# A graph attention kernel: VectorE's chain for the next chunk behind the second, third and fifth add, weights five groups ahead

## The chip, the cores and the metric

The kernel runs on one core of a Trainium2 chip. The metric is the device time of one execution in microseconds (us). The core has a matrix engine (TensorE, PE in the profile), a vector engine (VectorE, DVE), a scalar engine (ScalarE, ACT), a general engine that here mostly issues gathers (GpSimd, POOL) and an engine that issues transfers (SyncE, SP). They run their own instruction lists and meet at semaphores.

## What is computed

3125 nodes with 128 features, 50,000 edges sorted by their target node `dst`. First a layer norm and two plain graph convolutions, then a layer norm and five graph attention layers with two heads, each followed by relu but the last; both blocks add their input. Of the reference, the attention layer, which is where the change lies:

```python
def _gat_layer(x, src, dst, edge_attr_full, W, att, b, ew, eb):
    edge_emb = edge_attr_full @ ew.T + eb
    xw = x @ W
    xj = xw[src].reshape(-1, H, D) + edge_emb.reshape(-1, H, D)
    xi = xw[dst].reshape(-1, H, D)
    alpha = einsum('ehd,hd->eh', xi, att_i) + einsum('ehd,hd->eh', xj, att_j)
    alpha = leaky_relu(alpha, NEG_SLOPE)
    amax = segment_max(alpha, dst, num_segments=N)
    ea = exp(alpha - amax[dst])
    denom = segment_sum(ea, dst, num_segments=N)
    alpha = ea / (denom[dst] + EPS)
    msg = xj * alpha[..., None]
    aggr = segment_sum(msg, dst, num_segments=N)
    return aggr.mean(axis=1) + b
```

Every node also has an edge to itself, without attributes.

## The kernel before

The edges are cut into 391 tiles of 128 (one edge in each partition), the tiles into groups of four and the groups into chunks: 13 chunks of 28 tiles (seven groups), one of 16 and one of 11 tiles. That is 98 groups a layer and 490 in all. The 3125 nodes are 25 tiles.

**GpSimd** issues one indirect gather for each edge tile (L510): 128 rows of the layer's node table, picked by the edges' sources, go to one of 60 slots of `ring`. From the 60th tile on it first waits until TensorE has ended the group whose slot it fills (`sums`, L508). The gathers of a chunk count up one of five semaphores `gath`.

**TensorE** (`aggregate`) waits for a group's weights (`p_ready`), clears a bank with a zero matmul (L741) and multiplies each tile's gathered rows by the weighted one-hots `pw` (L745), and its edge attributes `est` by the plain one-hots (L747). The last one counts up `sums`. Behind the second, fourth and sixth group of chunks 0 to 7 (and the second of chunk 8) stands a self tile (L783): a node tile times the layer's weights, for the edges of nodes to themselves. It waits until VectorE has read the self tile before.

**VectorE** runs through a list that is written out by hand, chunk by chunk:
- `rescale` (L1185 to L1191) adapts the sums of the node that straddles two chunks;
- `add_group` (L1200), once for each group, waits for `sums` and adds a bank to the accumulators `acc`;
- `weigh` (L1161) makes the weights `pw` of a group that lies `AHEAD` groups further on in the same chunk;
- `self_rows` (L1215, L1216) takes a self tile out of its bank;
- the chain of the next chunk. `windows_sum` has three parts (L1087; L1091; L1093, L1094 and L1096). `chain_scan` (L1105 to L1123) waits until all gathers of the next chunk have landed, since it needs a column of the gathered rows, and forms the running maxima within 32 edges; `chain_rows` (L1129 to L1145) and `chain_cols` (L1150 to L1156) join them over the whole chunk; `chain_probs` (L1170 to L1175) waits for ScalarE's exponentials, writes `est` and weighs the next chunk's first two groups. At the end of a chunk `weigh` is called for the next chunk's groups 2 to `AHEAD`-1.

In `chain_at` stands behind which add of a chunk (counted from 0) the scan, the rows with the columns, and the probabilities go. There are six banks for the sums and six places for `pw` (`DEEP`).

**ScalarE** computes the exponentials (L586) and copies windows for the next chunk (L580). **SyncE** loads the attributes and the weights and stores the node table.

Of the kernel before, what the change touches and what calls it, by code (L numbers as in the profile page):

```python
# [49 lines left out]
GC = [[g for g in range(G) if GROUPS[g][0] == c] for c in range(NC)]  # L50
# [20 lines left out]
def s_tile_of(c, i):  # L71
    n = 3 * c + i // 2
    return n if c < 9 and i % 2 == 1 and i < 6 and n < NT else None
# [7 lines left out]
    return sum(not pool_group(k) for k in range(g + 1))  # L81


AHEAD = 4
SUM_BANKS = (0, 1, 2, 4, 5, 6)
DEEP = len(SUM_BANKS)


def chain_at(c):
    return (2, 3, 5) if len(GC[c]) >= 7 else (0, 1, len(GC[c]) - 2)  # L90


def in_class(c, layer):
# [4 lines left out]
def program(nc, x, src_rows, src_key, src_flat, dst_col, dst_next_col, dst_flat, dst_first,  # L98
            attr, W1, b1, W2, b2,
            weights, weightsT, attT, edge_w, edge_b, edge_woT, biases, edge_bias, out):  # L100
    with ExitStack() as ctx:
# [707 lines left out]
        def _(v):  # L809
# [7 lines left out]
            def link(ins):  # L817
                v.wait_ge(step, mark(ins))
# [110 lines left out]
            def weight_columns(layer):  # L929
                V.tensor_copy(Wl[:, layer % 2, H * D:H * D + H], V4[:, layer, 0:4:2]).then_inc(wv_sb, 1)  # L930
# [90 lines left out]
            for g in range(GCN_G):  # L1021
# [3 lines left out]
                c, i = divmod(g, K // GRP)  # L1025
# [55 lines left out]
            def windows_sum(layer, c, part):  # L1081
                gc, k, hk = layer * NC + c, CH[c], H * CH[c]
                ts = slice(TC[c], TC[c + 1])
                win, pr = ai_win[:, 0:k, :, :], prod[:, 0:hk * FA].rearrange("p (h k f) -> p h k f", h=H, f=FA)
                if part == 0:
                    v.wait_ge(at_in[gc % NAT], 16 * (gc // NAT + 1))
                    link(V.tensor_tensor(pr, at[:, gc % NAT, 0:k, :].unsqueeze(1).broadcast_to((P, H, k, FA)),  # L1087
                                         v17[:, layer, :, 0:FA].unsqueeze(2).broadcast_to((P, H, k, FA)), ALU.mult))
                if part == 1:
                    v.wait_ge(win_ready, gc + 1)  # L1090
                    link(V.tensor_tensor(win, win, onehot[:, ts, :].unsqueeze(2).broadcast_to((P, k, H, WIN)), ALU.mult))  # L1091
                if part == 2:
                    V.tensor_reduce(ee[:, 0:hk], prod[:, 0:hk * FA].rearrange("p (q f) -> p q f", f=FA), AX, ALU.add)  # L1093
                    link(V.tensor_reduce(alpha[:, :, 0:k].rearrange("p h k -> p k h"), win, AX, ALU.add))  # L1094
                    v.sem_inc(win_used, 1)
                    link(V.tensor_tensor(alpha[:, :, 0:k], alpha[:, :, 0:k],  # L1096
                                         ee[:, 0:hk].rearrange("p (h k) -> p h k", h=H), ALU.add))
# [27 lines left out]
            def chain_rows(layer, c):  # L1125
                k = CH[c]
                r = NQB * k
                for i in range(NQB):
                    V.tensor_copy(seq[:, :, i:r:NQB], endsT[i * QB:i * QB + H, :, 0:k])  # L1129
                if c == 0:  # L1130
                    V.memset(carry[:, 0, 1:2], -BIG)
                else:
                    V.tensor_copy(carry[:, 0, 1:2], carry[:, 0, NQB * CH[c - 1] + 1:NQB * CH[c - 1] + 2])
                link(V.memset(carry[:, 1, r:r + 1], -BIG))
                V.tensor_tensor_scan(carry[:, 0, 2:r + 2], seq[:, 2, 0:r], seq[:, 0, 0:r], carry[:, 0, 1:2],
                                     ALU.add, ALU.max)
                link(V.tensor_tensor_scan(carry[:, 1, 0:r][:, ::-1], seq[:, 3, 0:r][:, ::-1], seq[:, 1, 0:r][:, ::-1], -BIG,
                                          ALU.add, ALU.max))
                link(V.tensor_tensor(cmax[:, :], carry[:, 0, 1:2], carry[:, 1, 0:1], ALU.max))
                link(V.tensor_scalar(carry[:, 2, 1:P + 1], carry[:, 0, 1:2].broadcast_to((H, P)), cmax[:, :], None,  # L1140
                                     ALU.subtract))
                for i in range(NQB):
                    ins = V.tensor_copy(into[i * QB:i * QB + H, :, :], carry[:, :, 1 + i:1 + P:NQB])  # L1143
                link(ins)
                link(V.transpose(intoT[:, :, :], into[:, :, :]))  # L1145
# [12 lines left out]
            def weigh(layer, g):  # L1158
                c, t, n = GROUPS[g]
                k = t - TC[c]  # L1160
                V.tensor_tensor(pw[:, g % DEEP, 0:n, :, :],  # L1161
                                onehot[:, t:t + n, :].unsqueeze(2).broadcast_to((P, n, H, WIN)),
                                est[:, c % 2, k:k + n, HF:HF + H].unsqueeze(3).broadcast_to((P, n, H, WIN)), ALU.mult)\
                    .then_inc(p_ready, 1)

            def chain_probs(layer, c):
# [11 lines left out]
                v.wait_ge(step, done)  # L1178
                for g in GC[c][0:2 if c else AHEAD]:
                    weigh(layer, g)  # L1180

            def rescale(layer, c):
                base = window_bases(TC[c], 1)
                p0 = H * QB
                link(V.tensor_scalar(dd[:, p0 + H:p0 + REG], phi_mask[:, 0:1], dd[:, p0:p0 + 1], None, ALU.mult))  # L1185
                link(V.scalar_tensor_tensor(out=dd[:, p0 + H:p0 + REG], in0=phi_mask[:, 1:2], scalar=dd[:, p0 + 1:p0 + 2],
                                            in1=dd[:, p0 + H:p0 + REG], op0=ALU.mult, op1=ALU.add))
                if c:
                    v.wait_ge(added, layer * G + GC[c][0])
                col = acc[:, :, bass.ds(base[0], 1)]  # L1190
                link(V.tensor_tensor(col, col, dd[:, p0:p0 + REG].unsqueeze(2), ALU.mult))  # L1191

            def add_group(layer, g):
                _, t, n = GROUPS[g]
                base = window_bases(t, 1)
                if layer * G + g:
                    v.wait_ge(added, layer * G + g)
                v.wait_ge(sums, layer * G + g + 1)
                win = acc[:, :, bass.ds(base[0], GW)]
                V.tensor_tensor(win, win, grp_sum(g).rearrange("p (r w) -> p r w", r=REG), ALU.add)\  # L1200
                    .then_inc(added, 1)

            for layer in range(LAYERS):
# [9 lines left out]
                def self_rows(j):  # L1213
                    v.wait_ge(s_ps, n + j + 1)
                    V.tensor_copy(node_ai[:, :, j], bank[3][:, H * D:H * D + H])  # L1215
                    V.tensor_tensor(S[:, j, :], bank[3][:, 0:H * D], ebl[:, :], ALU.add)\  # L1216
                        .then_inc(s_sb, 1)
# [10 lines left out]
                for c in range(NC):  # L1228
                    more = c + 1 < NC
                    rescale(layer, c)  # L1230
                    scan_at, rows_at, probs_at = chain_at(c)
                    n_groups = len(GC[c])
                    for i, g in enumerate(GC[c]):
                        if more and scan_at >= 2 and i < 3:
                            windows_sum(layer, c + 1, i)
                        add_group(layer, g)
                        if i + AHEAD < n_groups:
                            weigh(layer, GC[c][i + AHEAD])
                        if s_tile_of(c, i) is not None:
                            self_rows(s_tile_of(c, i))  # L1240
                        if more and scan_at < 2 and i == 0:
                            for part in range(3):
                                windows_sum(layer, c + 1, part)
                        if more and i == scan_at:
                            chain_scan(layer, c + 1)
                        if more and i == rows_at:
                            chain_rows(layer, c + 1)
                            chain_cols(layer, c + 1)
                        if more and i == probs_at:
                            chain_probs(layer, c + 1)  # L1250
                        if more and i == n_groups - 1:
                            for ahead in GC[c + 1][2:AHEAD]:
                                weigh(layer, ahead)
                    if c == 10:
                        if not final:
                            weight_columns(layer + 1)
                        v.wait_ge(lay_e, 32 * (layer + 1))
                        V.tensor_tensor(El[0:EC, :], El[0:EC, :], Bl, ALU.add).then_inc(El_sum, 1)
# [119 lines left out]
```

## Time and profile before

| | us |
|---|---|
| median of 3 runs | 3388.01 |
| lowest, highest run | 3386.20, 3390.43 |
| span of the profiled execution | 3764.7 |
| busy: TensorE matmuls | 2439.0 |
| busy: VectorE | 2004.0 |
| busy: GpSimd | 2210.5 |
| busy: ScalarE | 696.7 |

The profiled execution's own time is its span, from the first instruction to the last. It is 376.7 us longer than the median of the runs without a profile, so durations and orders are read from it, and its waits are to be held against the runs' time. Times in rows are counted from the start of the span. In a row, `ring<-table,srci` reads: writes `ring`, reads `table` and `srci`; the bracket at the end tells how long the engine had been idle before the instruction and what ended that. Five attention layers lie in the span, the third from about 1180 to 1754 us.

### The profile page before, as it was taken

What the parts mean: (1) busy time and instruction counts of PE and PEld (TensorE: products, weight loads), DVE (VectorE), ACT (ScalarE), POOL (GpSimd) and SP (SyncE); (2) the same over time, 40 slices, a digit from 0 to 9 for tenths busy, and PEclk for the clock granted to TensorE, in tenths of its full rate; (3) what the DMA queues carried; (4) which work ended last, traced back from release to release, by engine and by line L of the source; (5) the groups of instructions that cost most, each with busy time, mean ns of one, the idle gap of its engine ahead of it and who ended that gap; (6) DMA issues with size and microseconds to landing.
All of it is one profiled execution on the core that took longest, in us unless ns stands there. A gap on an engine that the chain in (4) does not pass through costs nothing.

```text
span 3764.7 us, 48376 instructions
## 1 busy us (share of the span) xinstructions
PE 2439.0 (65%) x13595; PEld 2001.4 (53%) x13595; DVE 2004.0 (53%) x6216; ACT 696.7 (19%) x3102; POOL 2210.5 (59%) x2357
## 2 busy tenths in 40 slices
PE   6779726666582766658276665837576582766668
PEld 6679615555461655547165554725455461655546
DVE  8955624554472555547255554725454472555456
ACT  0078511111121111112111111211111121111112
POOL 0067466666626766662666666266676626666661
PEclk8555555555565555556555555655555565555556
DMA  3212122222202222221222222022222202222221
GB/s 101 97 60 80 30 52 54 53 52 57 49 24 51 54 51 53 56 49 30 47 54 52 53 56 49 25 53 54 50 53 57 50 24 50 54 50 53 52 49 40
DMA packets 114121, 195.78 MB, mean 52 GB/s; under 512 B 39897, under 2 KB 77272, under 8 KB 113864
## 3 DMA queue, kind: packets, MB, share of 16 engines
q0 software_dynamic: 62560, 130.25, 15.2%
q1 hardware_dynamic: 51304, 62.42, 5.3%
q8 instruction: 122, 2.00, 0.2%
q14 instruction: 135, 1.11, 0.1%
HBM read 180.86 MB, written 11.67 MB: 51 GB/s over the span
## 4 chain that ended last, share of the span: by engine, by line
DVE 36%; PE 25%; another core or an unknown queue 20%; issue 13%; DVEq 3%; POOL 1%; ACT 1%; ACTq 1%; DMA 0%; POOLq 0%
PE bank L745 10%; PE bank L747 6%; DVE acc L1200 4%; DVE into L1143 2%; DVEq L1016 2%; PE bank L718 2%; DVE pw L1161 2%; DVE alpha L1094 2%; PE bank L741 2%; PE bank L783 2%; DVE fwd L1150 2%; DVE lanes L1129 2%; DVE prod L1072 1%; PE bank L766 1%
## 5 line engine op out<-in xcount | busy, mean ns | idle before, releaser
L510 POOL DMA_INDIRECT ring<-table,srci x1955 | 1941.2, 993 | 937.6 <-issue 556.4
L745 PE MATMUL bank<-pw,ring 128*128 128x48 f32 x3910 | 1210.9, 404 | 203.3 <-issue 201.8
L745 PEld LDWEIGHTS bank<-pw,ring 128*128 128x128 f32 x3910 | 1014.9, 314 | 302.9 <-issue 231.1
L1200 DVE TENSOR_TENSOR acc<-acc,bank 128x288 f32 x490 | 222.8, 455 | 1128.7 <-remote 857.3
L747 PE MATMUL bank<-onehot,est 128*36 128x24 f32 x3910 | 632.6, 243 | 222.9 <-issue 221.7
L741 PE MATMUL bank<-zeros 128*128 128x288 bf16 x490 | 208.5, 426 | 697.1 <-DVE pw L1161 438.7
L747 PEld LDWEIGHTS bank<-onehot,est 128*36 128x36 f32 x3910 | 391.2, 149 | 393.9 <-issue 226.6
L741 PEld LDWEIGHTS bank<-zeros 128*128 128x128 bf16 x490 | 55.4, 113 | 752.0 <-DVE pw L1161 453.3
L586 ACT ACTIVATE dd<-dd 128x66 f32<-128x66 f32 x75 | 19.4, 258 | 2163.4 <-DVE dd L1154 1177.9
L580 ACT COPY ai_win<-ai_rows 128x48 f32 x1955 | 336.3, 229 | 432.6 <-issue 410.5
L491 POOL TENSOR_TENSOR ring<-ring,acc 128x512 f32<-128x512 f32 x98 | 117.1, 1195 | 250.1 <-ACT ring L545 246.7
L517 POOL TENSOR_TENSOR S<-S 128x128 f32<-128x128 f32 x125 | 57.4, 459 | 323.6 <-ACT S L590 319.2
L783 PE MATMUL bank<-Wl,S 128*128 128x258 f32 x250 | 152.8, 697 | 50.1 <-issue 48.7
L718 PE MATMUL bank<-onehot,ring 128*128 128x24 f32 x784 | 172.2, 388 | 18.4 <-ACT ring L556 7.9
L718 PEld LDWEIGHTS bank<-onehot,ring 128*128 128x128 f32 x784 | 169.3, 331 | 21.1 <-DVE bank L1043 8.8
L1091 DVE TENSOR_TENSOR ai_win<-ai_win,onehot 128x1344 f32<-128x1344 f32 (+2 forms) x75 | 109.1, 1455 | 122.5 <-issue 101.2
L1161 DVE TENSOR_TENSOR pw<-onehot,est 128x192 f32<-128x192 f32 x490 | 160.0, 352 | 0.1
L556 ACT ACTIVATE ring<-ring,acc 128x128 f32<-128x128 f32 x392 | 124.3, 389 | 29.4 <-PE bank L718 24.7
L1143 DVE COPY into<-carry 2x96 f32<-2x96 f32 x300 | 93.6, 312 | 45.9 <-issue 33.8
L800 PE MATMUL bank<-El,acc 128*128 128x256 f32 x250 | 95.8, 470 | 23.8 <-DVE y L1305 20.0
L1094 DVE TENSOR_REDUCE alpha<-ai_win 128x56 f32<-128x1344 f32 (+2 forms) x75 | 108.6, 1448 | 0.0
L783 PEld LDWEIGHTS bank<-Wl,S 128*128 128x128 f32 x250 | 64.6, 308 | 70.3 <-issue 63.8
(214 smaller groups left out, 2610.1 us busy)
## 6 DMA issues: line engine op xcount, KB each, us to landing
ring<-table,srci POOLq DMA_INDIRECT x1955
ai_rows<-lo_dram SPq DMA_DIRECT2D x28, 896.0 KB, 4.3
at<-in_attr SPq DMA_DIRECT2D x65, 224.0 KB
table<-ring SPq DMA_DIRECT2D x15, 390.0 KB, 3.5
table<-ring SPq DMA_DIRECT2D x5, 325.0 KB, 3.4
result<-ring SPq DMA_DIRECT2D x24, 64.0 KB
x_mid<-ring SPq DMA_DIRECT2D x3, 384.0 KB, 2.7
table<-ring SPq DMA_DIRECT2D x5, 130.0 KB, 2.4
```

The lines of the kernel that those rows point to most:

```text
L510: nc.gpsimd.indirect_dma_start(out=ring[:, slot(t), :], out_offset=None, in_=table, in_offset=bass.IndirectOffsetOnAxis(ap=srci[:, t:t + 1 ...
L556: ins = nc.scalar.activation(rows[:, g % 3, k, :], pre[:, g % 3, k, :], ACT.Relu, scale=n_e[:, t:t + 1])
L580: ins = nc.scalar.copy(ai_win[:, t - TC[c] + k, :, :], ai_rows[:, :, bass.ds(base[k], WIN)])
L718: ins = nc.tensor.matmul(total[:, at_k], rows[:, g % 3, k, :], onehot[:, t0 + k, :], start=False, stop=k == GRP - 1, skip_group_check=True)
L741: nc.tensor.matmul(total, zeros[:, 0:P], zeros[:, :], start=True, stop=False, skip_group_check=True)
L745: nc.tensor.matmul(wide[:, 0:H, at_k], ring[:, slot(t), 0:D], pw[:, g % DEEP, k, :, :], start=False, stop=False, skip_group_check=True)
L747: ins = nc.tensor.matmul(wide[0:EC, H, at_k], est[:, c % 2, t - TC[c], :], onehot[:, t, :], start=False, stop=k == n - 1, skip_group_check ...
L783: nc.tensor.matmul(bank[3][:, 0:H * D + H], S[:, j, D:2 * D], Wl[:, layer % 2, :], start=True, stop=True).then_inc(s_ps, 1)
L1094: link(V.tensor_reduce(alpha[:, :, 0:k].rearrange("p h k -> p k h"), win, AX, ALU.add))
L1143: ins = V.tensor_copy(into[i * QB:i * QB + H, :, :], carry[:, :, 1 + i:1 + P:NQB])
L1161: V.tensor_tensor(pw[:, g % DEEP, 0:n, :, :], onehot[:, t:t + n, :].unsqueeze(2).broadcast_to((P, n, H, WIN)), est[:, c % 2, k:k + n, HF:H ...
L1200: V.tensor_tensor(win, win, grp_sum(g).rearrange("p (r w) -> p r w", r=REG), ALU.add)\
```

## The change

Three numbers that set the order on VectorE, and the loop that uses them. For chunks of seven groups the scan of the next chunk goes behind the add with index 1 in place of 2, the rows and columns behind 2 in place of 3, the probabilities behind 4 in place of 5. `AHEAD` is 5 in place of 4. The first two parts of `windows_sum` both stand ahead of the first add and the third ahead of the second; before, one part stood ahead of each of the first three adds. The chunks of 16 and 11 tiles keep their order apart from `AHEAD`.

```diff
-AHEAD = 4
+AHEAD = 5
 SUM_BANKS = (0, 1, 2, 4, 5, 6)
 DEEP = len(SUM_BANKS)
...
 def chain_at(c):
-    return (2, 3, 5) if len(GC[c]) >= 7 else (0, 1, len(GC[c]) - 2)
+    return (1, 2, 4) if len(GC[c]) >= 7 else (0, 1, len(GC[c]) - 2)
...
                     for i, g in enumerate(GC[c]):
-                        if more and scan_at >= 2 and i < 3:
-                            windows_sum(layer, c + 1, i)
+                        if more and scan_at >= 1 and i < 2:
+                            for part in ((0, 1), (2,))[i]:
+                                windows_sum(layer, c + 1, part)
                         add_group(layer, g)
...
-                        if more and scan_at < 2 and i == 0:
+                        if more and scan_at < 1 and i == 0:
                             for part in range(3):
                                 windows_sum(layer, c + 1, part)
```

On VectorE, at the head of the first chunk of the first layer, behind `rescale` (L1191), the first two parts of the next chunk's windows (L1087, L1091) and the adds around them; - is before, + is after:

```order
 L1191 TENSOR_TENSOR acc<-acc,dd 128x3
 L1087 TENSOR_TENSOR prod<-at,v 128x896
-L1016 TENSOR_LOAD lanes
-L1200 ISA
-L1200 TENSOR_TENSOR acc<-acc,bank 128x3x96
-L1161 TENSOR_TENSOR pw<-onehot,est 128x192
 L1091 TENSOR_TENSOR ai_win<-ai_win,onehot 128x1344
 L1016 TENSOR_LOAD lanes
```

An add (L1200, with the load of its place, L1016, and its wait) and a weigh (L1161) no longer stand between L1087 and L1091.

On VectorE, in the second half of the same chunk, from the end of the next chunk's columns (L1156) to its probabilities (L1170), before:

```order
L1156 STREAM_TRANSPOSE maxes<-fwd 128x64
L1016 TENSOR_LOAD lanes
L1200 ISA
L1200 TENSOR_TENSOR acc<-acc,bank6 128x3x96
L1016 TENSOR_LOAD lanes
L1200 ISA
L1200 TENSOR_TENSOR acc<-acc,bank0 128x3x96
L1215 COPY node_ai<-bank3 128x2
L1216 TENSOR_TENSOR S<-bank3,ebl 128x256
L1170 STREAM_TRANSPOSE probs<-dd 128x64
```

And after, the same place:

```order
L1156 STREAM_TRANSPOSE maxes<-fwd 128x64
L1016 TENSOR_LOAD lanes
L1200 ISA
L1200 TENSOR_TENSOR acc<-acc,bank5 128x3x96
L1215 COPY node_ai<-bank3 128x2
L1216 TENSOR_TENSOR S<-bank3,ebl 128x256
L1016 TENSOR_LOAD lanes
L1200 ISA
L1200 TENSOR_TENSOR acc<-acc,bank6 128x3x96
L1170 STREAM_TRANSPOSE probs<-dd 128x64
```

The adds between the columns and the probabilities are those of the fourth and fifth group (banks 5 and 6) in place of the fifth and sixth (banks 6 and 0), and the self rows (L1215, L1216) stand between the two adds, not behind them.

## Rows read from the trace of the kernel before

**Rows 1.** The page: span, and the gathers' group (busy, mean ns, idle before).

```profile
span 3764.7 us, 48376 instructions
...
L510 POOL DMA_INDIRECT ring<-table,srci x1955 | 1941.2, 993 | 937.6 <-issue 556.4
```

**Rows 2.** Waits, whole span: us in total, times, longest us.

```profile
PE bank L741 <- DVE pw L1161: 438.7, 53, 68.8
...
POOL ring L510 <- remote: 288.6, 113, 8.4
...
POOL ring L510 <- PE bank L747: 53.7, 12, 12.8
```

**Rows 3.** Timeline, third layer, a chunk's border: start, us, engine, instruction.

```profile
1536.12 0.45 DVE L1200 TENSOR_TENSOR acc<-acc,bank 128x288 f32 x1 [6.34 <-remote]
...
1538.81 0.42 PE L741 MATMUL bank<-zeros 128*128 128x288 bf16 x1 [10.60 <-DVE pw L1161]
...
1542.22 0.42 PE L741 MATMUL bank<-zeros 128*128 128x288 bf16 x1
...
1546.66 0.45 PE L741 MATMUL bank<-zeros 128*128 128x288 bf16 x1
```

**Rows 4.** Timeline: first gathers of layers, chunk 12's first matmul, layers' last adds.

```profile
475.50 1.14 POOL L510 DMA_INDIRECT ring<-table,srci  x1 [21.93 <-DMA table<-ring]
...
1696.26 0.42 PE L741 MATMUL bank<-zeros 128*128 128x288 bf16 x1 [0.53 <-issue]
...
1748.14 0.46 DVE L1200 TENSOR_TENSOR acc<-acc,bank 128x288 f32 x1 [2.12 <-PE bank L747]
...
1790.18 0.97 POOL L510 DMA_INDIRECT ring<-table,srci  x1 [4.32 <-DMA table<-ring]
...
3726.20 0.45 DVE L1200 TENSOR_TENSOR acc<-acc,bank 128x288 f32 x1 [2.12 <-PE bank L747]
```

**Rows 5.** Timeline, first layer: chunk 0's last gather and its scan.

```profile
510.00 0.94 POOL L510 DMA_INDIRECT ring<-table,srci  x1 [0.30 <-issue]
...
512.64 0.26 DVE L1105 TENSOR_TENSOR alpha<-alpha,ring 128x56 f32<-128x56 f32 x1 [8.33 <-DMA ring<-table,srci]
...
514.73 0.22 DVE L1123 TENSOR_TENSOR fwd<-fwd,bwd 128x64 f32<-128x64 f32 x1
```

**Rows 6.** Timeline, third layer: VectorE around the rows and columns.

```profile
1521.60 0.22 DVE L1123 TENSOR_TENSOR fwd<-fwd,bwd 128x64 f32<-128x64 f32 x1
1522.38 0.45 DVE L1200 TENSOR_TENSOR acc<-acc,bank 128x288 f32 x1 [0.56 <-DVE fwd L1123]
...
1522.75 0.15 DVE L1215 COPY node_ai<-bank 128x2 f32<-128x2 f32 x1
...
1523.15 1.19 DVE L1129 COPY lanes<-endsT 2x112 f32<-2x112 f32 x4
...
1529.33 0.45 DVE L1200 TENSOR_TENSOR acc<-acc,bank 128x288 f32 x1 [0.55 <-issue]
...
1718.82 1.04 DVE L1200 TENSOR_TENSOR acc<-acc,bank 128x288 f32 x2 [0.56 <-DVE maxes L1156]
```

**Rows 7.** Timeline, third layer: probabilities, weighs, next windows, and a gather beside.

```profile
1537.40 1.08 DVE L1175 TENSOR_TENSOR est<-at,probs 128x896 f32<-128x896 f32 x1
1537.44 1.86 POOL L510 DMA_INDIRECT ring<-table,srci  x1 [0.30 <-issue]
1538.40 0.62 DVE L1161 TENSOR_TENSOR pw<-onehot,est 128x192 f32<-128x192 f32 x2
...
1538.94 0.45 DVE L1200 TENSOR_TENSOR acc<-acc,bank 128x288 f32 x1
...
1540.63 1.09 DVE L1087 TENSOR_TENSOR prod<-at,v 128x896 f32<-128x896 f32 x1
...
1542.49 0.46 DVE L1200 TENSOR_TENSOR acc<-acc,bank 128x288 f32 x1 [0.77 <-DVE prod L1087]
...
1543.16 1.55 DVE L1091 TENSOR_TENSOR ai_win<-ai_win,onehot 128x1344 f32<-128x1344 f32 x1
```

## The prediction

> **What bounds the kernel now.** I read the page first [rows 1]. GpSimd's gathers cost more than anything else in the layers: 1955 of them, 0.99 us each on average, with 0.30 us of issue between two, so one starts about every 1.25 us. The span is 3764.7 us, though, 376.7 us above the median of the runs, 3388.0 us, and the waits say where the profiled execution differs [rows 2]: the gathers stood 288.6 us for an event that the view calls "remote" and 53.7 us for TensorE's last matmul of a group, 342.3 us together. [Rows 3] show that the first of these are reports that come late: the zero matmul at 1538.81 had waited 10.60 us, so TensorE had ended all groups of the chunk before by 1528.21, yet the sixth add of that chunk stood for "remote" until 1536.12. I take this lateness to belong to the profiled execution and not to the timed ones. That is a choice; the check on it is a sum without it. Setup ends with the first gather at 475.50 [rows 4]. Chunks 0 to 12 of a layer hold 364 tiles, so the last gather of chunk 12 starts 363 x 1.25 = 453.8 us after the first if nothing holds the queue, 2.64 us later its chunk can be scanned (510.00 to 512.64, the one place where the scan waits for a transfer by the profile [rows 5]), some 18 us go to locks (below), 12.2 us from that scan to TensorE's start on chunk 12, and from there to the last add are 1748.60 - 1696.26 = 52.3 us [rows 4]: 538.9 us a layer. Four times 1790.18 - 1748.60 = 41.6 us lie between layers, and 3764.7 - 3726.65 = 38.1 us behind the last. In all 475.5 + 2694.5 + 166.4 + 38.1 = 3374.5 us, 13.5 us (0.4%) under the median. TensorE alone would need, per chunk, seven groups of 3.41 us (1538.81 to 1542.22) and up to three self tiles of 1.03 us (4.44 us from 1542.22 to 1546.66, less 3.41) [rows 3], 27 us against 28 x 1.25 = 35 us of gathers. So the plain run is bound by the gathers: VectorE's scan waits for the next chunk's last gather, TensorE waits for VectorE, and nothing holds GpSimd's queue but the **locks**.
>
> **The locks.** The gather at 1537.44 met VectorE's L1175 (1537.40, 1.08 us, both inputs in SBUF) and took 1.86 us in place of 0.95; it ended 0.82 us after L1175 did, although two more such operations (L1161) stood right behind [rows 7]. So a gather that starts inside such an operation goes on when that ends, and the next starts 0.82 + 0.30 = 1.12 us later. L1175, L1087 (1.09 us) and L1091 (1.55 us) do this; the adds and row sums, with one input in SBUF, I price at nothing, since the gathers at their times took 0.95. The Trainium skill ("SBUF — State Buffer", section "Who interferes with whom") has the lock, held for the whole instruction, but infers that a tensor_tensor does not stop the making of a DMA's descriptors; the 1.86 us beside 0.95 us speaks against that for these gathers.
>
> **The change part by part.** No instruction is added or removed in the loop and the order on TensorE, ScalarE and SyncE stays; only VectorE's order moves. *The scan behind the second add* does not come earlier: it waits for a gather. By then all seven groups are weighed either way (2+4 or 1+5 ahead), so the fifth weigh ahead, 0.27 us of VectorE's waiting time, buys TensorE nothing there. What is left is where the three long locks fall between the gathers. I put zero at L1105's start; the gathers then start at -2.64 + 1.25k. Steps: L1105 to L1123 2.09 [rows 5]; L1123 to an add 0.78, add to the next step 0.37, with self rows between 0.77; L1129 to the add behind the chain 6.18; add to add 0.59 (1.04 for two, one of them 0.45) [rows 6]; the last add before L1170 to L1175 1.28 with self rows [rows 3, 7], 0.88 without; L1175 to the first weigh 1.00, to the add 1.54; add to L1087 1.69 with two weighs, so 1.96 with three (0.54 for two); L1087 to L1091 2.53 before [rows 7], and 1.09 when they adjoin.
>
> Chunks 0 to 7 have self rows behind the adds after the scan. *Before*: add 2.87, L1129 3.64, adds 9.82 and 10.41, L1175 11.69 to 12.77, L1087 14.92 to 16.01, L1091 17.45 to 19.00. The gather at 12.36 is held, the next are at 13.89, 15.14 (held by L1087), 17.13, 18.38 (held by L1091) and 20.12. That is the 17th, due at 18.61 without locks: 1.51 us lost. *After*: add 2.87, L1129 3.24 (no self rows there), adds 9.42 and 10.19, L1175 11.07 to 12.15. The gather of 11.11 is held; then 13.27, 14.52, 15.77. TensorE now matters at one point: the self tile behind group 5 needs self rows that now stand behind the chain (they end near 10.27), so group 6 starts at 11.3 and its add, 3.68 us later (1538.81 to 1542.49 [rows 7, 3]), at 14.95, where VectorE would be ready at 13.4. L1087 is at 16.91 to 18.00 and L1091 to 19.55; the gathers of 17.02 and 19.12 are held, the next is at 20.67, again the 17th: 2.06 us lost. **+0.55 us a chunk**, eight times.
>
> Chunks 8 to 10 have none there. *Before*: L1175 10.89 to 11.97 (holds 11.11), L1087 14.12 to 15.21 (holds 14.34), L1091 16.65 to 18.20 (holds 17.58), next 19.32, the 16th, due 17.36: 1.96 lost. *After*: L1087 14.98 to 16.07 (holds 15.59), L1091 to 17.62 (holds 17.19), next 18.74: 1.38 lost. **-0.58 us**, three times. Hence the 18 us above: 8 x 1.51 + 3 x 1.96.
>
> A layer's start costs one weigh more, 0.27 us, on VectorE behind the first two, where TensorE has work. At its end TensorE works from 1696.26 on for seven times 3.41 us on chunk 12, and the chain of chunk 13, whose 16 gathers landed early, lies beside that; that it moves 3.4 us forward is worth from 0 to about 1 us a layer, and I take 0. The windows that L1091 reads are made by ScalarE right behind the exponentials, which keep their place. Sum: 8 x 0.55 - 3 x 0.58 = +2.7 us a layer, five layers +13.3 us: 3388.0 + 13.3 = **3401 us**. The steps are good to 0.1 us a chunk, 11 chunks and 5 layers: +-5.5, with the odd gather of the weighs some +-8: 3394 to 3410.
>
> **The rivals.** *A, the forecast.* 3401 us.
> *B, the other side: the gather of 11.11 slips ahead of L1175.* The margin is 0.04 us, and the 2.64 us of the landing is one reading. If the landing is 0.1 us longer, or L1175 0.1 us later, L1175 lies between the gathers of 11.11 and 12.36 and holds none; then come 13.61, 14.86, 16.11, 17.36 (held by L1087) and 19.12 (held by L1091), and the one of 20.67 is the 18th, due at 19.86: 0.81 lost, 0.70 fewer than before. 8 x (-0.70) - 1.7 = -7.3 a layer, -37 us: 3351. For it: that margin. Against: the single reading gives the hit, and a shorter landing gives it too.
> *C, a mix.* Landings vary by tenths and some chunks go one way, some the other; two in three as in A and one in three as in B leave 13.3 x 2/3 - 37/3 = -3.5: about 3385, from 3378 to 3395.
> *D, the late reports are real in plain runs.* Then a chain that stands one group (3.4 us) earlier on VectorE shortens TensorE's waits for the weights, 438.7 us in 53 waits [rows 2]. If only the 13.5 us that my sum misses are such waits, 3374; if every one of 55 boundaries gains 3.4 us, 3201. Against it: with the lateness the sum would be near 3765, and it isn't.
> *E, adjoining locks let no gather in between.* L1091 now starts where L1087 ends. If the gather held by L1087 had to wait for both, each of 11 chunks loses one place more, 55 x 1.25 = 69 us: 3470. Against it: at 1538.48 a gather did get in between L1175 and L1161 [rows 7].
> *F, the locks cost nothing.* Then the change does nothing that a plain run shows: 3388. By the page's inference this would be so; 1.86 us against 0.95 us speaks against it, and so do 993 ns as the mean of all gathers [rows 1], 0.05 us x 1955 = 90 us in all, as the sum has it (5 x 18).
>
> **How the numbers follow.** A 0.48, B 0.20, C 0.16, D 0.08, E 0.05, F 0.03. The likeliest gives 3401, its own range is 3394 to 3410. The range has to take in B, since A and C hold under two thirds: 3350 to 3412, which leaves out E, the far end of D and the edges of the others, under 2 in 10. A measurement of this kernel tells about 0.2% (6.8 us) from no change. Faster: B, D and 0.07 of C, 0.35. Same (3381 to 3395): 0.07 of C, F, and 0.05 of A, 0.15. Slower: the rest of A, E and 0.02 of C, 0.50.
>
> **What would show it.** In the profile after: the scan still ends its wait with the gathers' landing where it waits for one at all, the gathers stay 1.25 us apart but for locks, and their mean goes from 993 ns to some 1000 (A) or 975 (B). A held gather right at L1087's end would speak against E. The forecast is wrong if the time between gathers has changed with no lock beside it, if TensorE's zero matmul waits less for the weights in the same measure as the time falls (D), or if self rows behind the chain hold TensorE longer than its 10 us of slack per chunk.

## The result and the profile after

The changed kernel takes 3394.48 us (median of 20 runs, 3391.01 to 3398.66) against 3388.59 us before (20 runs, 3386.20 to 3393.12): **5.9 us more, a ratio of 1.0018, 95% interval 1.0012 to 1.0024**. The sign is clear of noise; the size lies just inside the 0.2% that the prediction set as no change. A better setting of the same edit exists: with weights four groups ahead in place of five it takes 3348 us, and with the locks below taken away the kernel takes 3295 to 3297 us in each of the three orders that were run. One execution of one of those kernels (locks away, chain of before) took 4607.5 us beside five of 3294 to 3295 us and is left out of its ratio.

The rows of before in the front were read from an execution with late reports. The same kernel was profiled again (first run below) with a span near the time of its plain runs, so the two pages to compare are these. Page of the changed kernel, span and groups (busy, mean ns of one | idle before, what ended most of it):

```profile
span 3390.2 us, 48441 instructions
...
L510 POOL DMA_INDIRECT ring<-table,srci x1955 | 1964.2, 1005 | 632.6 <-issue 590.3
...
L741 PE MATMUL bank<-zeros 128*128 128x288 bf16 x490 | 209.6, 428 | 428.4 <-DVE pw L1161 428.4
L1105 DVE TENSOR_TENSOR alpha<-alpha,ring 128x56 f32<-128x56 f32 (+7 forms) x75 | 18.1, 242 | 809.5 <-DMA ring<-table,srci 809.0
...
L783 PE MATMUL bank<-Wl,S 128*128 128x258 f32 x250 | 153.6, 717 | 414.7 <-DVE S L1216 414.7
```

And of the kernel before, profiled again:

```profile
span 3392.7 us, 48376 instructions
...
L510 POOL DMA_INDIRECT ring<-table,srci x1955 | 1967.3, 1006 | 633.9 <-issue 570.8
...
L741 PE MATMUL bank<-zeros 128*128 128x288 bf16 x490 | 209.6, 428 | 646.6 <-DVE pw L1161 646.6
...
L1105 DVE TENSOR_TENSOR alpha<-alpha,ring 128x56 f32<-128x56 f32 (+7 forms) x75 | 18.2, 242 | 766.1 <-DMA ring<-table,srci 765.9
...
L783 PE MATMUL bank<-Wl,S 128*128 128x258 f32 x250 | 153.6, 717 | 198.2 <-DVE S L1216 198.2
```

Against [rows 1, 2]: the "remote" waits of the gathers are gone in both, and VectorE's scan waits for gathers, 766 and 809 us in all. The change shifts TensorE's waiting (218 us less for weights, 217 us more for the self rows), lets VectorE wait 43 us more at the scans and shifts nothing else of size. What sets the time is the gathers' busy time: it differs by 3 us here, and the spans by 2.5.

That these two single executions point the other way than the medians has a reason that lies outside the kernels. Two gathers that nothing holds start 1.252 us apart (median) in the second page and 1.249 us apart in the first. Over 1955 gathers that makes 5 to 6 us, so with equal distances the changed kernel's span would be the longer one. The distance does not go with the kernel: it is 1.252 us in the four profiles of the first series of runs below and 1.249 us in the seven of the other two series, in which both chains stand.

One usual chunk after the change, VectorE, TensorE's group and the gathers on the timeline (start, us):

```profile
658.11 0.94 POOL L510 DMA_INDIRECT ring<-table,srci  x1 [0.30 <-issue]
...
660.66 0.26 DVE L1105 TENSOR_TENSOR alpha<-alpha,ring 128x56 f32<-128x56 f32 x1 [11.65 <-DMA ring<-table,srci]
...
663.92 1.05 DVE L1129 COPY lanes<-endsT 2x112 f32<-2x112 f32 x4
...
665.60 1.05 POOL L510 DMA_INDIRECT ring<-table,srci  x1 [0.30 <-issue]
...
671.59 1.08 DVE L1175 TENSOR_TENSOR est<-at,probs 128x896 f32<-128x896 f32 x1
...
671.96 1.54 POOL L510 DMA_INDIRECT ring<-table,srci  x1 [0.30 <-issue]
...
675.59 0.46 DVE L1200 TENSOR_TENSOR acc<-acc,bank 128x288 f32 x1 [1.62 <-PE bank L747]
...
677.56 1.09 DVE L1087 TENSOR_TENSOR prod<-at,v 128x896 f32<-128x896 f32 x1
...
677.70 1.77 POOL L510 DMA_INDIRECT ring<-table,srci  x1 [0.30 <-issue]
...
678.69 1.56 DVE L1091 TENSOR_TENSOR ai_win<-ai_win,onehot 128x1344 f32<-128x1344 f32 x1
...
679.77 1.29 POOL L510 DMA_INDIRECT ring<-table,srci  x1 [0.30 <-issue]
```

Counted from the scan, L1175 stands at 10.93, the add that waits for TensorE at 14.93, L1087 at 16.90 and L1091 at 18.03; the prediction had 11.07, 14.95, 16.91 and 18.00. Each of the three holds a gather, which takes 1.54, 1.77 and 1.29 us in place of 0.94. The scan starts 2.55 us after the start of the gather it waits for (660.66 less 658.11).

### The profile page after: what moved, and what is told of

Same layout as the page of the kernel before. It is cut to its first block, busy times and chain, and to the rows that moved or that the text cites. A ratio compares the mean times of both kernels' runs of the same rounds, so it can differ in the third digit from the quotient of the medians.

```text
span 3390.2 us, 48441 instructions
## 1 busy us (share of the span) xinstructions
PE 2402.4 (71%) x13595; PEld 1981.8 (58%) x13595; DVE 1992.1 (59%) x6216; ACT 669.5 (20%) x3102; POOL 2233.1 (66%) x2357
## 4 chain that ended last, share of the span: by engine, by line
POOL 52%; issue 18%; DVE 15%; PE 12%; DMA 1%; ACT 1%; DVEq 1%; POOLq 0%; ACTq 0%
POOL ring L510 49%; PE bank L745 5%; PE bank L747 3%; POOL ring L491 2%; DVE prod L1072 2%; DVE ring L847 2%; PE bank L718 1%; DMA ring<-table,srci 1%; PE bank L741 1%; DVE y L1300 1%; DVE y L1306 1%; DVE ai_rows L940 1%; POOL ring L486 1%; DVE into L1143 1%; DVE prod L1270 1%
## 5 line engine op out<-in xcount | busy, mean ns | idle before, releaser
L510 POOL DMA_INDIRECT ring<-table,srci x1955 | 1964.2, 1005 | 632.6 <-issue 590.3
L747 PE MATMUL bank<-onehot,est 128*36 128x24 f32 x3910 | 619.1, 246 | 0.0
L1105 DVE TENSOR_TENSOR alpha<-alpha,ring 128x56 f32<-128x56 f32 (+7 forms) x75 | 18.1, 242 | 809.5 <-DMA ring<-table,srci 809.0
L747 PEld LDWEIGHTS bank<-onehot,est 128*36 128x36 f32 x3910 | 382.6, 150 | 177.5
L783 PE MATMUL bank<-Wl,S 128*128 128x258 f32 x250 | 153.6, 717 | 414.7 <-DVE S L1216 414.7
L1200 DVE TENSOR_TENSOR acc<-acc,bank 128x288 f32 x490 | 221.7, 452 | 284.5 <-PE bank L747 131.4
L580 ACT COPY ai_win<-ai_rows 128x48 f32 x1955 | 309.1, 228 | 57.9 <-issue 22.7
L1161 DVE TENSOR_TENSOR pw<-onehot,est 128x192 f32<-128x192 f32 x490 | 153.9, 350 | 0.0
L1091 DVE TENSOR_TENSOR ai_win<-ai_win,onehot 128x1344 f32<-128x1344 f32 (+2 forms) x75 | 109.6, 1462 | 27.3 <-ACT ai_win L580 25.1
```

Of the source, the lines that this page charges most:

```text
L510: nc.gpsimd.indirect_dma_start(out=ring[:, slot(t), :], out_offset=None, in_=table, in_offset=bass.IndirectOffsetOnAxis(ap=srci[:, t:t + 1 ...
L580: ins = nc.scalar.copy(ai_win[:, t - TC[c] + k, :, :], ai_rows[:, :, bass.ds(base[k], WIN)])
L747: ins = nc.tensor.matmul(wide[0:EC, H, at_k], est[:, c % 2, t - TC[c], :], onehot[:, t, :], start=False, stop=k == n - 1, skip_group_check ...
L783: nc.tensor.matmul(bank[3][:, 0:H * D + H], S[:, j, D:2 * D], Wl[:, layer % 2, :], start=True, stop=True).then_inc(s_ps, 1)
L1161: V.tensor_tensor(pw[:, g % DEEP, 0:n, :, :], onehot[:, t:t + n, :].unsqueeze(2).broadcast_to((P, n, H, WIN)), est[:, c % 2, k:k + n, HF:H ...
```

## The experiments

In what follows "lost" is the time from the start of one chunk's last gather to that of the next chunk's last, less 28 times the distance of two gathers that nothing holds in the same profile (1.252 us in the first series, which is the first four runs below; 1.249 us in the changed kernel's profile and in the second and third series, four and three runs). It is counted over the 55 stretches between the scans that VectorE does in chunks 0 to 11 of each layer: 40 have self rows behind the scan, 15 have none. Each ratio is to the kernel before as run in the same series, 3391.0, 3386.5 and 3388.4 us.

**The kernel before once more.** No edit.

> The kernel before once more, for a profile whose span is near the time of the plain runs. Lock theory: 3388 us, a span near it, the scan L1105 waits some 11 us in each chunk for the gathers, GpSimd waits for nothing but issue between gathers, and chunks with self rows behind the scan lose about 1.5 us to locks, those without about 2.0 us. Rival (TensorE's new wait for self rows costs the 6 us): the same time, and locks that lose as much as in the changed kernel.

3390.72 us, ratio 0.9998 (0.9988 to 1.0008). The chunk that answers to the one above:

```profile
659.66 0.26 DVE L1105 TENSOR_TENSOR alpha<-alpha,ring 128x56 f32<-128x56 f32 x1 [10.68 <-DMA ring<-table,srci]
...
663.31 1.32 DVE L1129 COPY lanes<-endsT 2x112 f32<-2x112 f32 x4
...
671.52 1.08 DVE L1175 TENSOR_TENSOR est<-at,probs 128x896 f32<-128x896 f32 x1
672.09 1.34 POOL L510 DMA_INDIRECT ring<-table,srci  x1 [0.30 <-issue]
...
673.73 1.13 POOL L510 DMA_INDIRECT ring<-table,srci  x1 [0.31 <-issue]
...
674.75 1.09 DVE L1087 TENSOR_TENSOR prod<-at,v 128x896 f32<-128x896 f32 x1
675.17 1.50 POOL L510 DMA_INDIRECT ring<-table,srci  x1 [0.30 <-issue]
...
677.28 1.55 DVE L1091 TENSOR_TENSOR ai_win<-ai_win,onehot 128x1344 f32<-128x1344 f32 x1
...
678.22 1.43 POOL L510 DMA_INDIRECT ring<-table,srci  x1 [0.30 <-issue]
```

All as expected: the scan waits 10.7 us, and the chunks lose 1.59 us with self rows and 1.92 us without (medians; forecast 1.51 and 1.96). In the changed kernel it is 2.07 and 1.43 (forecast 2.06 and 1.38). The gather of 673.73 took 1.13 us: it met the two weighs behind the add, which the prediction's sum had put at nothing. Here that costs nothing, since L1087 holds the next gather with or without it.

**Five groups ahead alone.**

```diff
-AHEAD = 4
+AHEAD = 5
```

> Only the weights five groups ahead, the chain where it was. Lock theory: a third weigh ahead of L1087 moves it 0.27 us back, to 2.42 us behind L1175's end, where the second gather behind the lock starts at 2.37 us: that gather slips ahead of L1087 by 0.05 us, each of 11 chunks loses 0.98 us less, 54 us in all: 3335 us; if it is held after all, 0.27 us more a chunk: 3403 us. Rival (self rows and TensorE): neither stands elsewhere than before, so 3388 us.

3389.41 us, ratio 0.9995 (0.9986 to 1.0004): neither of the two numbers of the lock theory, and the trace says why.

```profile
671.76 1.08 DVE L1175 TENSOR_TENSOR est<-at,probs 128x896 f32<-128x896 f32 x1
672.33 1.34 POOL L510 DMA_INDIRECT ring<-table,srci  x1 [0.30 <-issue]
...
673.97 1.13 POOL L510 DMA_INDIRECT ring<-table,srci  x1 [0.30 <-issue]
...
675.26 1.09 DVE L1087 TENSOR_TENSOR prod<-at,v 128x896 f32<-128x896 f32 x1
675.41 1.77 POOL L510 DMA_INDIRECT ring<-table,srci  x1 [0.30 <-issue]
...
678.76 1.16 POOL L510 DMA_INDIRECT ring<-table,srci  x1 [0.30 <-issue]
```

L1087 stands 2.42 us behind L1175's end (672.84), as expected. The gather does not stand at 2.37 but at 2.57 us, because the weighs held the one ahead of it (1.13 us); so L1087 catches it at its start, it takes 1.77 us, and the next, at L1091, loses 0.27 us less than before (1.16 against 1.43). The two nearly cancel in the chunks with self rows: 1.63 us lost in place of 1.59. The rival's number fits, but not its reason.

**The windows alone.**

```diff
-                        if more and scan_at >= 2 and i < 3:
-                            windows_sum(layer, c + 1, i)
+                        if more and scan_at >= 1 and i < 2:
+                            for part in ((0, 1), (2,))[i]:
+                                windows_sum(layer, c + 1, part)
...
-                        if more and scan_at < 2 and i == 0:
+                        if more and scan_at < 1 and i == 0:
```

> Only the windows moved: L1087 and L1091 adjoin ahead of the first add, the chain and four groups ahead as before. Lock theory: L1175 and L1087 stand as before, L1091 starts at 16.0 in place of 17.45 us after the scan and holds the gather of 17.13: 0.2 us less lost a chunk, 10 us in all: 3378 us. Rival (self rows and TensorE): 3388 us.

3386.48 us, ratio 0.9988 (0.9979 to 0.9997), 4 us less. The chunks with self rows lose 1.47 in place of 1.59 us, the others 1.80 in place of 1.92: a gain of 0.12 us each where 0.2 was expected. The sign is the lock theory's, the size small.

**The chain and windows as changed, four groups ahead.**

```diff
-AHEAD = 5
+AHEAD = 4
```

> The chain and the windows as in the changed kernel, four groups ahead. Lock theory: the seventh group is weighed behind the scan, so L1175 starts 0.27 us later, near 11.3 us after the scan, between the gathers of 11.2 and 12.5: in chunks with self rows it holds none, and one gather more fits; 3351 us if all 8 chunks a layer do so, 3375 us if half do. Rival (self rows and TensorE): self rows and the wait of TensorE for them stand as in the changed kernel, or 0.27 us later: 3394 us or a little more.

**3347.66 us**, ratio 0.9873 (0.9858 to 0.9888): 43 us faster than before, and by the two ratios some 49 us faster than the changed kernel. The seventh group's weigh behind the scan puts L1175 at 11.38 us behind the scan, and the gathers lie on either side of it:

```profile
657.53 0.26 DVE L1105 TENSOR_TENSOR alpha<-alpha,ring 128x56 f32<-128x56 f32 x1 [10.44 <-DMA ring<-table,srci]
...
668.73 0.96 POOL L510 DMA_INDIRECT ring<-table,srci  x1 [0.30 <-issue]
...
668.91 1.08 DVE L1175 TENSOR_TENSOR est<-at,probs 128x896 f32<-128x896 f32 x1
...
669.99 1.08 POOL L510 DMA_INDIRECT ring<-table,srci  x1 [0.30 <-issue]
```

Chunks with self rows lose 0.93 us, the others 0.24. The second number was not expected: in the 15 chunks without self rows, too, L1175 holds no gather, and of the 48 us that all 55 stretches lose less than before (47.0 in place of 94.7) these fifteen make 23. TensorE's wait for self rows is nearly as long as in the changed kernel (388.5 against 414.7 us), so this wait does not cost the time: the rival falls.

**A delay ahead of the probabilities.** The changed kernel, and in `chain_probs` of full chunks a row sum whose result is not used:

```diff
+                if c and k == K:
+                    V.tensor_reduce(ee[:, 0:18], prod[:, 0:18 * FA].rearrange("p (q f) -> p q f", f=FA), AX, ALU.add)
                 v.wait_ge(exp_al, gc + 1)
```

> The changed kernel with one idle row sum of some 0.36 us more on VectorE ahead of each full chunk's probabilities; its result is not used. Lock theory: L1175 starts near 11.35 us after the scan, between the gathers of 11.2 and 12.5, as it does with four groups ahead, and in spite of 55 operations more the time falls to about 3350 us. Rival (the order of adds and self rows, or work on VectorE, sets the time): 3394 us or up to 20 us more.

3354.44 us, ratio 0.99 (0.9883 to 0.9916). More work on VectorE, placed to shift L1175 by some 0.3 us, makes the changed kernel 40 us faster; chunks with self rows lose 0.84 us, those without 1.61.

**Four more L1087, and four more row sums, where VectorE waits.** In the kernel before, ahead of `chain_scan`:

```diff
+                        if more and i == scan_at and n_groups >= 7 and CH[c + 1] == K:
+                            for _ in range(4):
+                                windows_sum(layer, c + 1, 0)
```

> The kernel before, with L1087 done four times more, 60 times in all, just ahead of the scan, where VectorE waits 10.7 us for the gathers; the same values are written again. Lock theory: gathers that start in such an operation wait for its end, so in 4.4 us two are done in place of three or four: about 1.9 us a chunk, 60 chunks: 3390 + 115 us, from 3465 to 3540 us. Rival (what VectorE does while it waits for gathers costs nothing): 3390 us.

and with `link(V.tensor_reduce(ee[:, 0:H * K], prod[...], AX, ALU.add))` in place of `windows_sum(layer, c + 1, 0)`:

> The kernel before, with the row sum L1093 (1.05 us, one input) done four times more at the same 60 places. Lock theory: one input in SBUF holds no gather, 3390 us. Rival (any work on VectorE beside the gathers holds them): as much as four more L1087 cost, some 3500 us.

The multiplications cost 77 us: 3463.95 us, ratio 1.0226 (1.0209 to 1.0243). The row sums, as long, cost nothing: 3385.59 us, ratio 1.0000 (0.9991 to 1.0010). The gathers' group of the page with the multiplications, and, from its timeline, one such place:

```profile
L510 POOL DMA_INDIRECT ring<-table,srci x1955 | 2038.9, 1043 | 632.4 <-issue 569.2
...
1514.10 4.46 DVE L1087 TENSOR_TENSOR prod<-at,v 128x896 f32<-128x896 f32 x4
...
1514.30 1.70 POOL L510 DMA_INDIRECT ring<-table,srci  x1 [0.30 <-issue]
...
1516.31 0.94 POOL L510 DMA_INDIRECT ring<-table,srci  x1 [0.30 <-PE bank L747]
...
1517.56 1.82 POOL L510 DMA_INDIRECT ring<-table,srci  x1 [0.30 <-issue]
```

and the page with the row sums (L1246):

```profile
L510 POOL DMA_INDIRECT ring<-table,srci x1955 | 1961.0, 1003 | 633.5 <-issue 572.4
...
L1246 DVE TENSOR_REDUCE bwd<-prod 128x56 f32<-128x896 f32 x240 | 260.2, 1084 | 6.3
```

The gathers' busy time is 78 us longer with the first than with the second (2038.9 less 1961.0, both of one series), as the kernel's time is; with the second it is no longer than in the kernel before (1967.3). A chunk with self rows loses 1.3 us more than before and one without 1.7 (2.86 less 1.59, 3.63 less 1.92), where 1.9 were expected: the second gather here starts at the border of two operations and goes through in 0.94 us. VectorE was idle at the place in both, so it is not its time that is paid.

**The locks taken away.** On the run with four groups ahead: the factors of L1087 and L1175 in PSUM, and L1091 in parts of seven tiles.

```diff
-        probs = sb("probs", [P, H, QB])
+            probs = bank[7][:, 0:H * QB].rearrange("p (h e) -> p h e", h=H)
+            v_ps = bank[7][:, 128:128 + H * FA].rearrange("p (h f) -> p h f", h=H)
...
-                                         v17[:, layer, :, 0:FA].unsqueeze(2).broadcast_to((P, H, k, FA)), ALU.mult))
+                                         (v_ps if c else v17[:, layer, :, 0:FA]).unsqueeze(2).broadcast_to((P, H, k, FA)), ALU.mult))
...
-                    link(V.tensor_tensor(win, win, onehot[:, ts, :].unsqueeze(2).broadcast_to((P, k, H, WIN)), ALU.mult))
+                    for a in range(0, k, 7):
+                        z = min(k, a + 7)
+                        ins = V.tensor_tensor(win[:, a:z], win[:, a:z],
+                                              onehot[:, TC[c] + a:TC[c] + z, :].unsqueeze(2)
+                                              .broadcast_to((P, z - a, H, WIN)), ALU.mult)
+                    link(ins)
...
+                v.wait_ge(tr_sb, NQ * (layer + 1))
+                link(V.tensor_copy(v_ps, v17[:, layer, :, 0:FA]))
                 chain_probs(layer, 0)
```

> The changed chain with four groups ahead, and the locks taken away where that goes: the small factors of L1087 and L1175 are read from PSUM in place of SBUF, and L1091 is cut into four operations of seven tiles. Lock theory: of the 47 us that the locks of full chunks cost with four groups ahead, some 20 are left, 3320 us, from 3305 to 3335. Rival (length of the operation counts, not where its inputs are): L1087 and L1175 hold gathers as before, no less than 3340 us.

**3296.60 us**, ratio 0.9733 (0.9717 to 0.9749), better than expected. The page and the timeline (L1089 is what was L1087, L1182 what was L1175, L1095 what was L1091):

```profile
L509 POOL DMA_INDIRECT ring<-table,srci x1955 | 1862.5, 953 | 633.0 <-issue 582.7
...
670.18 1.09 DVE L1089 TENSOR_TENSOR prod<-at,bank 128x896 f32<-128x896 f32 x1
...
670.73 0.95 POOL L509 DMA_INDIRECT ring<-table,srci  x1 [0.30 <-issue]
...
671.30 1.76 DVE L1095 TENSOR_TENSOR ai_win<-ai_win,onehot 128x336 f32<-128x336 f32 x4
...
671.98 1.06 POOL L509 DMA_INDIRECT ring<-table,srci  x1 [0.30 <-PE bank L746]
```

The multiplication is as long as it was, 1.09 us, and the gather that starts in its middle takes 0.95 us. It is the place of the second input that held it, not the length. Of the 47 us that the 55 stretches lost with four groups ahead, 13 are left; some 20 were expected.

**The same edit on the chain of before and on the changed kernel, and cutting alone.** The first two have the edit above; the third cuts L1087, L1091 and L1175 into four operations of seven tiles each, with four groups ahead and all inputs in SBUF.

```diff
+                    for a in range(0, k, 7):
+                        z = min(k, a + 7)
+                        ins = V.tensor_tensor(pr[:, :, a:z], at[:, gc % NAT, a:z, :].unsqueeze(1).broadcast_to((P, H, z - a, FA)),
+                                              v17[:, layer, :, 0:FA].unsqueeze(2).broadcast_to((P, H, z - a, FA)), ALU.mult)
+                    link(ins)
```

> The kernel before (chain behind the third, fourth and sixth add, four groups ahead), with the small factors of L1087 and L1175 in PSUM and L1091 in four parts. Lock theory: without the long locks it does not matter where the chain stands, so 3297 us, within 7 us of the same edit on the changed chain. Rival (the earlier chain is worth something of its own, hidden so far by the locks): 10 us or more over the run with the changed chain.

> The changed kernel (chain behind the second, third and fifth add, five groups ahead) with the same edit. Lock theory: 3297 us, within 7 us of the run with four groups ahead and of the one with the chain of before. Rival (five groups ahead cost something of their own): 3 to 10 us more than with four.

> The changed chain with four groups ahead; L1087, L1091 and L1175 are each cut into four operations of seven tiles, and all inputs stay in SBUF. Lock theory: a held gather goes on when the short operation ends, so each loses at most about 0.35 us, some 0.45 us a chunk: 3310 us, from 3300 to 3325. Rival (adjoining operations hold a gather through to the end of the last): no gain, 3347 us or more.

3294.76 us (0.9724, 0.9711 to 0.9736), 3295.42 us (0.9725, 0.9713 to 0.9738) and 3309.60 us (0.9770, 0.9755 to 0.9784). Without the locks the chain of before, the changed one and the one with four groups ahead lie within 2 us. The first two are of one series and differ by 0.7 us, less than their runs scatter: **no effect of the change is left when the locks are gone**, so the 5.9 us came through them. Cutting alone gives most of the gain, so an operation that adjoins another does let a gather in.

All pages but the first of before, with its late reports, side by side; gathers' busy time against the span:

| kernel | runs, us | span | gathers busy | rest |
|---|---|---|---|---|
| before, profiled again | 3390.7 | 3392.7 | 1967.3 | 1425.4 |
| changed | 3394.5 | 3390.2 | 1964.2 | 1426.0 |
| five ahead alone | 3389.4 | 3384.2 | 1958.9 | 1425.3 |
| windows alone | 3386.5 | 3383.7 | 1957.8 | 1425.9 |
| chain changed, four ahead | 3347.7 | 3345.5 | 1914.9 | 1430.6 |
| changed, with delay | 3354.4 | 3352.3 | 1924.6 | 1427.7 |
| before, four more L1087 | 3464.0 | 3463.6 | 2038.9 | 1424.7 |
| before, four more row sums | 3385.6 | 3382.9 | 1961.0 | 1421.9 |
| locks away, chain of before | 3294.8 | 3292.5 | 1861.9 | 1430.6 |
| locks away, changed | 3295.4 | 3294.5 | 1862.4 | 1432.1 |
| locks away, four ahead | 3296.6 | 3295.4 | 1862.5 | 1432.9 |
| all three cut | 3309.6 | 3306.9 | 1871.8 | 1435.1 |

The span moves over 171 us and the rest over 13: to within some 13 us, what a lock adds to the gathers it adds to the kernel.

## Why the prediction was right, point by point

*What bounds the kernel.* Right. The late reports of [rows 2, 3] did belong to that one profiled execution; profiled again, the kernel's span is 3392.7 us, and the gathers' 634 us of idle time are issue and the layers' starts. The sum's 3374.5 us was 0.4% short, as it said.

*The locks.* Right: 77 us for four multiplications against nothing for four row sums, and 0.95 us beside a multiplication whose factor is in PSUM. The Trainium skill ("SBUF — State Buffer", section "Who interferes with whom") names the two SBUF inputs and the lock for the whole instruction, and the runs agree (1.70 and 1.82 us in place of 0.94); that a tensor_tensor leaves descriptor making alone, which the section infers, they speak against for these gathers.

*The chunks with self rows: +0.55 us.* The direction was right, the size nearly. A chunk in which L1175 holds its gather loses 2.07 us after (forecast 2.06) and 1.59 before (forecast 1.51): +0.48. The step that was off is VectorE's way to L1175 in the kernel before. Behind self rows the four copies of L1129 take 1.32 us (663.31), not the 1.19 of the one row read [rows 6], and 1.05 us without self rows ahead of them (663.92, after). So L1091 stands at 17.68 us in the kernel before (median), 0.23 behind the forecast, and at 18.08 in the changed one, 0.08 behind. The gather that follows L1091 starts about 1.1 us behind its end in both, so this is what the loss depends on. The shorter landing (2.55 us, not the one reading of 2.64) takes back 0.1 us in both.

*The margin.* That L1175 meets its gather at all hung on 0.04 us in the prediction. In nine of the 40 chunks it is 0.04 to 0.05 us; in most others it is some 0.35 (671.59 to 671.96 above), because an earlier gather was itself held for 0.1 us (665.60, 1.05 us). The prediction had one reading to decide it by, so that most chunks fell on the forecast's side was in part luck.

*The chunks without: -0.58 us.* Right: 1.92 to 1.43, -0.49.

*TensorE's wait for the self rows.* Right in place and length (the add 14.93 us behind the scan, forecast 14.95). It costs nothing by itself; it only sets where L1087 comes.

*The rivals.* B, the gather that slips ahead of L1175, happened in 5 of the 40 chunks of the profiled execution, where VectorE was late by some tenths; in two more a gather slipped ahead of L1087. One of the five:

```profile
708.89 0.94 POOL L510 DMA_INDIRECT ring<-table,srci  x1 [0.30 <-issue]
...
709.06 1.08 DVE L1175 TENSOR_TENSOR est<-at,probs 128x896 f32<-128x896 f32 x1
...
710.13 1.09 POOL L510 DMA_INDIRECT ring<-table,srci  x1 [0.30 <-issue]
```

This chunk lost 1.03 us, the one before it 2.05. With four groups ahead 35 of the 40 do so. So the forecast's mechanism and the rival's were one, some 0.3 us apart on VectorE. That the time with four groups ahead, 3348 us, is close to B's 3351 is partly chance: half of that gain came from the chunks without self rows, which B left as in A.

What came is A with a bit of C. In the two profiled executions the 40 stretches with self rows lose 78.5 us after and 65.8 before, +12.7, and the 15 without 21.1 and 28.9, -7.8: +4.9 us, where the runs say +5.9. The term that was mis-sized is that of the self-row chunks, 22 us in the sum (40 x 0.55) where 12.7 came. About 6 of the missing 9 us are the seven chunks in which a gather slipped (1.22 us lost on average, not 2.07), which the forecast had left to C; the other 3 are the 0.48 in place of 0.55. How many chunks slip in the executions that were not profiled isn't known. D fell: no gather waits for a late report in any of the pages above, and TensorE's 218 us less of waiting for weights bought nothing. E fell: the gather of 677.70 ended at 679.47, 0.82 us behind L1087's end (678.65), with L1091 running. F fell with the four multiplications.

*What the profile should show.* The gathers' mean was to go from 993 to some 1000 ns; it is 1005, but 993 was of the execution with late reports, and profiled again the kernel before has 1006. An effect of 5 us is 2.5 ns of this mean, as much as the two pages differ for gathers that nothing holds, so the mean can't tell A from no change here; the timeline by chunks can.

*Open.* Why the first profiled execution had late reports isn't known; no run brought them back. What makes VectorE late in the chunks in which a gather slips was not looked into; the run with the delay shows only that such a lateness is enough. Why gathers start 1.252 us apart in one series and 1.249 in the others isn't known either.

## What to carry to other kernels

When one engine's queue is never idle, price an edit on another engine by what it does to that queue: here, by where three long operations fall between gathers that start every 1.25 us. A gain or a loss that hangs on tenths of a microsecond of phase is better removed than tuned: two operands moved to PSUM and one long operation cut gave 2.7% in each of three orders, and cutting alone 2.3% in the one order that was run, where the order alone gave anything from +0.2% to -1.3%. A profile whose span lies 11% above the runs is worth taking again before its waits are believed. And before two profiles are compared to a few microseconds, compare in both an operation that the change does not touch, here a gather that nothing holds.

## What had not been expected of the hardware

A gather is held only by the operation that runs when it starts. 203 gathers start inside L1087, L1091 or L1175 before and 200 after the change. Seven of these had started in the operation's first 0.03 us and weren't held (0.94 us); seven others had started in its last 0.08 us. None of the rest ended later than 0.83 us behind the operation's end, whatever adjoined it. So cutting without any gap is enough, 3348 to 3310 us. Operations as short as a weigh (0.35 us) hold a gather too, by up to 0.2 us. And one kernel had profiled spans of 3764.7 and 3392.7 us with plain runs that agree to 0.2%.
